# A four-layer graph network on one core: last weights ahead of the scan, turned rows in pairs, other pick patterns

## The reference

```
h = maximum(layernorm(x), 0)
# layer 0, per edge: 48 + 48 + 32 inputs -> 128 -> 48
msg = relu(concat(h[dst], h[src], edge_attr_32) @ W1 + b1) @ W2 + b2
x   = x + segment_sum(msg, dst)
# layer 3, per edge: 48 + 48 + 16 inputs -> 128 -> 128 -> 48
m   = relu(relu(concat(h[src], h[dst], edge_attr_16) @ W1 + b1) @ W2 + b2) @ W3 + b3
x   = x + h + segment_sum(m, dst) / maximum(count, 1)
```

## Time and profile before

| what | value |
|---|---|
| runs, median (lowest to highest) | 7810.49 us (7810.36 to 7810.7) |
| the profiled execution | 7818.96 us |
| its span, first to last instruction | 7817.2 us |
| granted TensorE clock, mean | 0.941 of 2.4 GHz |
| busy share: PE, POOL, DVE, ACT | 84%, 75%, 66%, 27% |
| layer 0, first gather after the scatter to the first fetch of last rows | 319.87 to 2103.32 us |
| layer 3, the same | 5788.99 to 7682.30 us |

### The profile page before, as it was taken

The page is one execution under the profiler, slowest core; times in us unless marked ns, Lnnn a source line. Parts: engine busy times, 40 slices in busy tenths (PEclk is TensorE's granted clock), DMA queues, the critical chain, the costliest instruction groups (busy, mean ns, idle before and its releaser), DMA issues.

```text
span 7817.2 us, 86861 instructions
## 1 busy us (share of the span) xinstructions
PE 6592.4 (84%) x29118; PEld 5417.0 (69%) x29118; DVE 5178.3 (66%) x6239; ACT 2085.1 (27%) x5004; POOL 5843.9 (75%) x6133
## 2 busy tenths in 40 slices
PE   0399999999759999999579999999139999999992
PEld 0288888888647777777467777777127777777771
DVE  6377777777667777777777777777546666566663
ACT  5133333333212222222310000000014444444441
POOL 7777777777677777777767777777777777777776
PEclk9999999999879999999689999999669999999996
DMA  8255555555423334334223333333124444444442
GB/s 320 70 112 113 112 112 113 113 111 113 88 59 82 82 83 86 83 82 86 58 59 74 78 75 74 74 77 75 43 57 100 98 98 97 97 100 98 98 98 45
DMA packets 1062200, 721.34 MB, mean 92 GB/s; under 512 B 583026, under 2 KB 969508, under 8 KB 1061636
## 3 DMA queue, kind: packets, MB, share of 16 engines
q1 hardware_dynamic: 848144, 509.74, 23.9%
q0 software_dynamic: 197520, 163.66, 15.0%
q10 hardware_dynamic: 16100, 42.39, 1.4%
HBM read 477.71 MB, written 237.49 MB: 91 GB/s over the span
## 4 chain that ended last, share of the span: by engine, by line
POOL 47%; PE 32%; issue 16%; DVE 4%; DMA 2%; ACT 0%; POOLq 0%; SPq 0%; DVEq 0%; ACTq 0%
POOL G L669 39%; PE pRows L978 9%; PE pOdd L891 8%; POOL R L688 5%; PE pEven L891 3%; POOL first_rows L630 3%; PE pEven L958 2%; PE pT L946 2%; PE pOdd L958 2%; PE pRows L891 2%; DVE onehot L1256 1%; DVE S L1305 1%; DMA block_dst<-in_dst_dram,block_idx 1%; PE pOdd L883 0%; PE pEven L965 0%
## 5 line engine op out<-in xcount | busy, mean ns | idle before, releaser
L669 POOL DMA_INDIRECT G<-table,idx x2939 | 2785.7, 948 | 895.9 <-issue 882.7
L669 POOL DMA_INDIRECT G<-table,e_dst x2497 | 2365.8, 947 | 790.8 <-issue 754.6
L1199 DVE TENSOR_TENSOR_SCAN K<-mask_f,K,pT 48x512 f32<-48x512 bf16 x782 | 1005.5, 1286 | 1341.6 <-PE pT L946 1232.0
L978 PEld LDWEIGHTS pRows<-w,S 128*128 128x128 f32 x6256 | 1573.8, 324 | 307.2 <-issue 179.3
L891 PE MATMUL pOdd<-h_high,onehot 128*128 128x480 f32 (+1 forms) x3880 | 1520.4, 392 | 0.0
L891 PE MATMUL pOdd<-h_low,onehot 128*128 128x480 f32 (+1 forms) x3880 | 1491.4, 384 | 0.0
L978 PE MATMUL pRows<-w,S 128*128 128x48 f32 x6256 | 1445.7, 375 | 2.5 <-ACT O L824 0.5
L946 PE MATMUL pT<-ident,G 128*112 128x128 f32 x3128 | 478.9, 276 | 651.3 <-DMA G<-first_rows 327.4
L891 PE MATMUL pRows<-h_high,onehot 128*128 128x480 f32 (+1 forms) x2430 | 953.4, 392 | 84.9 <-DVE h_low L1052 84.9
L946 PEld LDWEIGHTS pT<-ident,G 128*112 128x112 f32 x3128 | 374.5, 134 | 808.1 <-DMA G<-table,idx 398.4
L891 PE MATMUL pRows<-h_low,onehot 128*128 128x480 f32 (+1 forms) x2430 | 920.8, 379 | 0.0
(11 more groups left out here) (203 smaller groups left out, 8433.3 us busy)
## 6 DMA issues: line engine op xcount, KB each, us to landing
mask_f<-same_row SPq DMA_DIRECT2D x392, 256.0 KB, 3.3
prefix<-O SPq DMA_DIRECT2D x194, 512.0 KB, 3.6
G<-first_rows SPq DMA_DIRECT2D x784, 96.0 KB
prefix<-O SPq DMA_DIRECT2D x390, 192.0 KB
G<-table,idx POOLq DMA_INDIRECT x2939
G<-table,e_dst POOLq DMA_INDIRECT x2497
first_rows<-zeros ACTq DMA_DIRECT2D x14, 2688.0 KB, 15.5
K<-in_ea_dram SPq DMA_DIRECT2D x588, 64.0 KB
```

Of the source, the lines that this page charges most:

```text
L669: pool.indirect_dma_start(rows[:, slot, j, 0:widths[l]], None, table[l], bass.IndirectOffsetOnAxis(ap=at[:, n, j:j + 1], axis=0))\
L978: last = pe.matmul(o, s[:, :, j], (w2_0 if l == 0 else w3_3)[:, :], start=True, stop=True)
L1199: dve.tensor_tensor_scan(K[r, c.slot, :], mask_of(c, r), pT[c.slot % 2][r, :], K[r, (c.slot - 1) % RING, CHUNK - 1:CHUNK], ALU.mult, ALU.add)\
```

## The change

In layers 0 and 3:
- The last weights are multiplied ahead of the scan: `time_rows` at lag 2, one product with the weights as the stationary operand and the 512 relu'd columns moving. Even chunks go to PSUM partitions 0 to 47, odd ones to 64 to 111. Relu writes to S in SBUF for it.
- The scan (lag 3 instead of 2) runs on these 48 rows and writes to `acc`, a ring of three pairs. Its carry comes from the other half of the partitions, so a small copy brings it over first (`carried_row`), and DVE waits for that copy.
- `turn_rows` at lag 4, once per pair: four transposes of 112 x 128, again over every fourth column. `copy_rows` follows at lag 4, two copies per pair.
- Picks: layer 0 in places 0, 2, 4 of every 7 chunks from chunk 12, layer 3 in one of every 4 from chunk 12. Their products are spread over two chunks, and the lag is 4 in both.
- PSUM banks are shared out anew; layer 3 has one bank for the first and one for the second layer, where it had two each.

```diff
-EDGE_PICK_CYCLE = {0: 3, 3: 6}
-EDGE_PICK_LAG = {0: 5, 3: 6}
+EDGE_PICK_CYCLE = {0: (7, (0, 2, 4)), 3: (4, (0,))}
+EDGE_PICK_LAG = 4
+EDGE_PICK_STEPS = 2
...
+        first_bank = {0: pH1, 3: [pH1[0]]}
+        second_bank = pH2[0]
+        edge_sum = {0: [pH2[1], pH2[0]], 3: [pH2[1], pH1[1]]}
+        turned_rows, timed_rows = pO
+        TURN = HIGH + D
...
 def copy_rows(c, l=l):
+    if not ends_pair(c):
+        return
+    first, turn = c.n // 2 * 2, c.turn
+    act.wait_ge(rows_made[l], c.n // 2 + 1)
+    if first >= RING:
+        act.wait_ge(rows_stored[c.pair], ((0 if l == 0 else TURNS) + turn) * 16)
+    for n in range(first, c.n + 1):
+        at = n % 2 * HIGH
+        last = act.activation(O[:, n % RING, 0:TJ * D].rearrange("p (j d) -> p j d", d=D),
+                              turned_rows[:, 0:TJ * TURN].rearrange("p (j w) -> p j w", w=TURN)
+                              [:, :, at:at + D], ACT.Copy)
+    last.then_inc(rows_copied[l], 1)
...
 def layer_2(c, l=l):
     pe.wait_ge(relu1[l], c.n + 1)
-    if not (c.fixed and c.n < 2):
+    if c.n >= 1:
+        pe.wait_ge(relu2[l], c.n)
...
-def make_rows(c, l=l):
-    for j in range(TJ):
-        o = rows_bank[l][c.n % len(rows_bank[l])][:, j * w:(j + 1) * w]
-        last = pe.matmul(o, s[:, :, j], (w2_0 if l == 0 else w3_3)[:, :], start=True, stop=True)
+def time_rows(c, l=l):
+    pe.wait_ge((relu1 if l == 0 else relu2)[l], c.n + 1)
+    if c.n >= 2:
+        pe.wait_ge(scanned[l], c.n - 1)
+    at = c.n % 2 * HIGH
+    pe.matmul(timed_rows[at:at + D, :], (w2_0 if l == 0 else w3_3)[:, :], S[:, c.slot % 4, :],
+              start=True, stop=True).then_inc(rows_timed[l], 1)
+def turn_rows(c, l=l):
+    if not ends_pair(c):
+        return
+    pair = c.n // 2
+    pe.wait_ge(scanned[l], c.n + 1)
+    if pair >= 1:
+        pe.wait_ge(rows_copied[l], pair)
+    rows = acc[0:TURN, pair % 3, :].rearrange("k (p j) -> k p j", j=TJ)
+    for j in range(TJ):
+        last = pe.transpose(turned_rows[:, j * TURN:(j + 1) * TURN], rows[:, :, j], ident[0:TURN, 0:TURN])
+    last.then_inc(rows_made[l], 1)
...
-stages = {0: [(0, transpose_rows), (1, layer_1), (3, make_rows), (0, sum_edge_pick)],
-          3: [(0, transpose_rows), (1, layer_1), (3, make_rows), (1, layer_2), (0, sum_edge_pick)]}[l]
+stages = {0: [(0, transpose_rows), (1, layer_1), (2, time_rows), (4, turn_rows), (0, sum_edge_pick)],
+          3: [(0, transpose_rows), (1, layer_1), (2, time_rows), (4, turn_rows), (1, layer_2),
+              (0, sum_edge_pick)]}[l]
...
 def scan(c, l=l):
+    dve.wait_ge(rows_timed[l], c.n + 1)
+    if c.at_pair_start and c.n >= 6:
+        dve.wait_ge(rows_made[l], c.n // 2 - 2)
+    at, pair = c.n % 2 * HIGH, c.n // 2
+    r = slice(at, at + D)
+    carry_in = 0.0
+    if c.n >= 1:
+        dve.wait_ge(scanned[l], c.n)
+        of = HIGH - at
+        link(dve.tensor_copy(carried_row[r, :], acc[of:of + D, (c.n - 1) // 2 % 3, CHUNK - 1:CHUNK]))
+        carry_in = carried_row[r, :]
+    dve.tensor_tensor_scan(acc[r, pair % 3, :], mask_of(c, r), timed_rows[r, :], carry_in, ALU.mult, ALU.add).then_inc(scanned[l], 1)
...
+if l in MLP:
+    link(dve.memset(acc[32:HIGH, :, :].rearrange("p a n -> p (a n)"), 0.0))
```

More of the change, by code:

```diff
@@ L46 @@
 QUADS = P // QUAD
+HIGH = 64
 PICK_SPAN = 10
@@ L64, in edge_picks @@
 def edge_picks(l, chunks):
-    return list(range(RING + EDGE_PICK_LAG[l], chunks, EDGE_PICK_CYCLE[l]))
+    cycle, places = EDGE_PICK_CYCLE[l]
+    first = RING + EDGE_PICK_LAG
+    return [n for n in range(first, chunks) if (n - first) % cycle in places]
 class Chunk:
@@ L256, in build @@
         place_of["S3"] = place_of["S"] + 3 * 4 * CHUNK
+        acc = over("e_w", "e_all", "acc", [P, 3, CHUNK], f32)
+        carried_row = over("pick_id_i", "pick_id", "carried_row", [P, 1], f32)
         h_high = over("e_all", "e_halves", "h_high", [P, B, D], f32r)
@@ L407, in gathered_by, with ends_pair @@
             return 16 * (before_l + sum(len(gathers_of(l, n)) for n in range(c.slot, c.n + 1, RING)))
+        def ends_pair(c):
+            return not c.at_pair_start or c.n + 1 == NCH
         def block_of(c):
@@ L788, in relu_1 @@
                     act.wait_ge(hidden1[l], c.n + 1)
-                    bank = pH1[c.slot % 2]
+                    bank = first_bank[l][c.n % len(first_bank[l])]
                     if l == 0:
-                        act.activation(bank[:, :], bank[:, :], ACT.Relu, bias=b1_0[:, :]).then_inc(relu1[l], 1)
+                        if c.n >= 4:
+                            act.wait_ge(rows_timed[l], c.n - 3)
+                        act.activation(S[:, c.slot % 4, :], bank[:, :], ACT.Relu, bias=b1_0[:, :]).then_inc(relu1[l], 1)
                         return
@@ L799, in relu_2 @@
                     act.wait_ge(hidden2[l], c.n + 1)
-                    bank = pH2[c.slot % 2]
-                    act.activation(bank[:, :], bank[:, :], ACT.Relu, bias=b2_3[:, :]).then_inc(relu2[l], 1)
+                    if c.n >= 4:
+                        act.wait_ge(rows_timed[l], c.n - 3)
+                    act.activation(S[:, c.slot % 4, :], second_bank[:, :], ACT.Relu, bias=b2_3[:, :])\
+                       .then_inc(relu2[l], 1)
                 def weight_rows(d, l=l):
@@ L819, in copy_rows @@
                 def copy_rows(c, l=l):
[L820 to L827, removed]
+                    if not ends_pair(c):
[10 more added lines that the diff above has]
+                    last.then_inc(rows_copied[l], 1)
+                stages = {0: [(0, copy_src), (1, relu_1), (4, copy_rows)],
+                          3: [(0, copy_src), (1, relu_1), (4, copy_rows), (1, relu_2)]}
                 if l in MLP:
@@ L953, in layer_1 @@
                         pe.wait_ge(ea_in[c.pair], (c.turn + 1) * 32 if l == 0 else TURNS * 32 + (c.turn + 1) * 16)
-                    if not (c.fixed and c.n < 2):
-                        pe.wait_ge(relu1[l] if l == 3 else scanned[l], c.n - 1)
+                    if c.n >= len(first_bank[l]):
+                        pe.wait_ge(relu1[l], c.n - len(first_bank[l]) + 1)
                     k = KROWS[l]
                     w = w1_0 if l == 0 else w1_3
-                    pe.matmul(pH1[c.slot % 2][:, :], w[0:k, :], K[0:k, c.slot, :], start=True, stop=True)\
+                    pe.matmul(first_bank[l][c.n % len(first_bank[l])][:, :], w[0:k, :], K[0:k, c.slot, :], start=True, stop=True)\
                       .then_inc(hidden1[l], 1)
```

47 lines of the change are left out of this document (18 added, 29 removed).

## The result

The changed kernel takes **7916.43 us** (median of 4 runs, 7912.65 to 7916.92) against 7810.42 for the kernel before, a ratio of 1.0134 (95% interval 1.0121 to 1.0147). It is slower by 1.3%; the forecast was 7722 us. Its profiled execution is 7916.92 us round a span of 7915.0 us, 97.8 us longer than the span before.

The account below looks back on a forecast made before the run. POOL's gathers, 1.25 us each, were taken as the pace, with PE nearly equal. Fewer gathers (86.2 us) and shorter drains (3 us) gave 89 us off the median of 7810.49: 7722 us, range 7714 to 7772.

Parts of the forecast that it names:

- PE's sum: PE in layer 0: seven chunks cost 28.6 us (ends 25.8 and 30.2), under POOL's 31.2.
- one 512-column product with the last weights: PE, layer 0, added per chunk: priced like the first layer's row, 0.54 us with its bubble, ends 0.43 and 0.77.
- "No stall" on DVE: The turn's wait for DVE's scan: worst scan ends at 5.7 us, PE comes to the turn at about 6.0.
- The turn: PE, four strided transposes added per pair: 1.07 us, priced like the removed loads, ends 0.49 and 1.07.
- Picks, copies, POOL: More picks leave 2870 gathers, still 1.25 us apart, saving 86.2 us if POOL stays the pace.
- The drain: Time after a layer's last gather starts: 1.5 us gained per layer, 3 us together; ends -3 and +4 each.
- Rival 1: PE stays last in layer 3 through exposed relu waits and 0.24 us bubbles: 34 us more, 7756; chance 0.12.
- Rival 2: 782 small DVE copies hold up gathers, one in four costing 0.25 us: 49 us, 7771; chance 0.07.
- Rival 3: PE's clock drops in layer 3's steps without picks; low in 70% of cycles costs 220 us, 7942; chance 0.11.
- Rival 4: Fewer gathers do not show because landing, stores or masks pace the chunks at the old rate: 7810; chance 0.04.
- 0.85 for "faster": Chance that the change is faster: forecast 0.66, rival 1 0.12, rival 2 0.07.

Follow-up runs that it names:

- 2: Changed kernel with PSUM banks dealt anew and the last weights' operand widened from 48 to 112 columns: 7760.66 us, ratio 0.9936.
- 4: Changed kernel with the 48-column products of both chunks of a pair issued two in a row, every second step: 7822.54 us, ratio 1.0017.
- experiment 6: Changed kernel with the 112-column operand, its PSUM banks, and DVE's scan ahead of placing and marking picks: 7732.67 us, ratio 0.9889.

## Why the prediction was wrong

**The step that failed** is a term of PE's sum: "one 512-column product with the last weights", priced by the first layer's row at 0.54 us "with its bubble", ends 0.43 and 0.77. It costs 2.05 - 0.54 = 1.51 us where it stands, nearly twice the upper end. Of the 0.97 us that the sum had too little, 0.65 is the width (2.05 against 1.40 with 112 columns); the other 0.32 is there with the wide operand too, 0.24 to 0.25 us idle in front of each of its two loads, so even that one (0.86 us) lies over my upper end. I compared the moving side alone (512 columns, two passes) and not the stationary one: 48 columns, where every other operand of these layers has 112 or 128. Seven chunks of layer 0 measured so are 7 x (0.55 + 1.06 + 0.99) + 3.5 x 0.46 + 3 x 4.24 (a pick's two steps, 2.06 and 2.18 by their starts) = 18.2 + 1.6 + 12.7 = 32.5 us, over POOL's 31.2 instead of 28.6. The trace agrees: PE's transposes of G in the 300 chunks that begin from 600 to 2000 us are 4.66 us apart, 32.6 per seven. The runs that remove only the pauses (2, and 4 by halving their number) bring layer 0 to 1733 and 1736 us.

The Trainium skill has a rule that fits, and I did not weigh it. "TensorEngine Tiling (Array Packing)", section "Key Properties", says that a change of tiling mode, though not of tile, drains TensorE, and its section "Tiling Modes" gives a mode of 128 rows by 64 columns. The runs agree where they touch it: 64 columns pay and 80 do not, and two products at two offsets in a row pay once. The section "Key Properties" also says that tiles work beside one another, which fits the 0.01 to 0.04 us of the second product. The price is 0.76 us in front and 0.82 behind, where other changes of operand show 0.24 to 0.28 or nothing. The runs show the condition and the price. That a product with at most 64 columns puts the array into another mode, and that the pause is this draining, is my inference from that page; no run shows it.

**"No stall" on DVE was wrong** in layer 3. I followed the turn's wait for the scan and not the one of `time_rows`, which comes earlier in PE's step: the product of chunk n waits for the scan of n - 2, done in the step before, behind place and mark. It cost 97.4 us in 94 waits; moving the scan gave 94.8 us of layer 3 back. In layer 3 the pauses matter less than in layer 0. I take the reason to be that they lie in front of a wait for relu (the second layer's load still waits for ACT 189 times, up to 0.8 us), which no run shows by itself. Cured alone the order gives 94.8 us there and the width 65.5, both together 104.5, not their sum. In layer 0 it is the other way round: 11.8, 87.1 and 85.0.

**The turn** was priced at 1.07 us a pair, with the removed loads' 0.267 each. It takes 0.46 behind the narrow product and 0.77 behind the wide one; its loads are 213 ns, not 324. That error is on the other side, 2.1 us per seven chunks, and hid part of the first.

**Picks, copies, POOL.** Right: 2870 gathers, 1.25 us apart where nothing holds them. The mechanism of the forecast holds as soon as both cures are in: experiment 6 has the two streams to within 0.4 us, and its ratio times 7810.4 is 7724, against 7722. The drain was forecast to shrink by 1.5 us a layer; with PE ahead it shrinks by 2.4 and 2.1, with PE behind it grows by 12.5 and 17.9, a term that I had bounded at 4.

**The rivals.** Rival 1 (PE stays last in layer 3) had the right engine, but left out layer 0, and its price was 34 us over the forecast for layer 3, where that layer is 102.7 us longer than in experiment 6, because it looked for bubbles of 0.24 us and had "1.1 us of slack". Rival 2: gathers are 947 ns beside 780 copies of 147 ns; nothing. Rival 3: the clock is 1.00 in both windows, and in experiment 6, where PE waits for gathers, 1.00 from 345 to 2040 and from 5780 to 7560 us as well; nothing. There was more for it than I wrote, though: I had read the end of layer 3 before the change as a stretch that "stayed at 1.00", from one slice of 5 us. Thirty us earlier the kernel before shows this row:

```profile
7630.00:7640.00 10.00, 10.00 (x33) 6.77 (x32) 4.52 (x4) 3.57 (x7) 7.57 (x8) 0.60 0.32 75
```

The granted clock is 0.60 there, near the 1.2 GHz level, after PE's loads had waited 1.66 and 2.24 us for gathers in the two steps before, with the second layer in each. Rival 4: excluded by POOL's waits for PE and by the time, which is 1.3% over the 7810 that it gives. So no case on my list was slower for the right reason, and 0.85 for "faster" leaned on one unmeasured row.

## What to carry to other kernels

When a matmul is added, find a row of before whose stationary operand has a like number of columns; if there is none, its price is open, and it should be bounded by hand against the slack. An operand of 48 or 64 columns between wider ones cost 0.65 us more here per visit than one of 112; widening it to 80 or 112 columns took the pauses away, and two narrow products in a row halved their number. And when a new wait enters a step, list every instruction that waits for the same engine, and put the work that others wait for ahead of the work that nobody waits for yet.

## What was unexpected of the hardware

- The pause at a change between operands of 48 or 64 and of 80 or more columns: 0.76 us in front and 0.82 behind, at the 2.4 GHz level, shown as PEld's "issue" and invisible in PE's busy time (99% of layer 0's window with it, 98% in experiment 6 without).
- A turn of 112 rows loaded from every fourth float takes 213 ns a load, where the old products' operand with the same stride and 128 rows took 324 ns. Whether rows or what stands around them make the difference was not tried.
- Two products of 48 columns at offsets 0 and 64, one behind the other, take 1.00 to 1.03 us with the pause behind them, one alone 0.99.
- The wide product has 0.24 to 0.25 us idle in front of each of its two loads and takes 0.85 us, not my 0.54; why was not tried.
